# Layer 1's norms of seven token groups moved from a stage of their own into the slots of the first products

## What is computed

```python
def _layernorm(x, axis=-1, eps=1e-05):
    m = jnp.mean(x, axis=axis, keepdims=True)
    v = jnp.var(x, axis=axis, keepdims=True)
    return (x - m) / jnp.sqrt(v + eps)
...
xn = _layernorm(x)
s = _L1_attn_ref(xn, ...)      # rms norm of xn, gate, linear recurrence over the sequence
g = _silu(_L1_ffn_ref(xn, ...))
x = x + s * g
...
# _L1_attn_ref
xn = x * jax.lax.rsqrt(jnp.mean(x * x, axis=-1, keepdims=True) + EPS) * norm_w
u = (xn @ in_w.T + in_b) * sigmoid(xn @ gate_w.T + gate_b)
# b, c, d are linear in u; h[t] = a * h[t-1] + b[t]; s = x + (c * h + d) @ out_w.T + out_b
...
# _L1_ffn_ref: switch-head attention, 8 heads of 64, 5 experts each, the 3 best kept
ss_g, sd_g = sigmoid(x @ Ws) * top3_mask, sigmoid(x @ Wd) * top3_mask
q, k, v = (sum over 5 experts of (x @ W_expert) * gate)  # per head
attn = softmax(q * scale @ k.T); out = attn @ v
```

## Time and profile before

| | |
|---|---|
| three runs | 2652.54, 2656.14, 2662.70 us; median 2656.14 |
| profiled execution | 2662.89 us, its span 2661.1 us |
| PE busy | 2414.3 us (91% of the span), 13848 matmuls |
| DVE busy | 1819.5 us (68%) |
| ACT busy | 1290.4 us (48%) |
| POOL busy | 1252.5 us (47%) |
| chain that ended last | PE 34%, DVE 8%, ACT 4%, POOL 3% |

### The profile page before, as it was taken

How to read it: one execution, slowest core, us unless ns; L and a number is a source line. 1 busy time by engine, 2 the same in 40 slices (tenths; PEclk the granted TensorE clock), 3 DMA queues, 4 the chain that set the end, 5 groups by cost and what they waited for, 6 DMA issues and landing times.

```text
span 2661.1 us, 39371 instructions
## 1 busy us (share of the span) xinstructions
PE 2414.3 (91%) x13848; PEld 1556.9 (59%) x13848; DVE 1819.5 (68%) x3844; ACT 1290.4 (48%) x3379; POOL 1252.5 (47%) x1120
## 2 busy tenths in 40 slices
PE   6688699999999999996899999999989889898888
PEld 3476345555555555555455666666544567677776
DVE  5767676777877778764688787887665666555723
ACT  4577523343343433433456777766556335454442
POOL 1654077777777777773267334341000642333430
PEclk7799799999999999997899999999998998889998
DMA  4464300000000000002822223232101360212113
GB/s 175 138 202 149 106 1 1 1 1 1 1 1 1 1 1 1 1 1 82 218 64 72 73 73 84 74 83 59 33 1 41 104 179 22 68 31 63 42 44 101
DMA packets 189332, 158.81 MB, mean 60 GB/s; under 512 B 101408, under 2 KB 168480, under 8 KB 188320
## 3 DMA queue, kind: packets, MB, share of 16 engines
q1 hardware_dynamic: 166352, 90.25, 12.7%
q0 software_dynamic: 22784, 66.05, 8.0%
HBM read 126.49 MB, written 59.51 MB: 70 GB/s over the span
## 4 chain that ended last, share of the span: by engine, by line
PE 34%; DVE 8%; ACT 4%; POOL 3%; issue 2%; DMA 1%; SPq 0%; POOLq 0%; ACTq 0%; DVEq 0%
PE bank L65 29%; PE bank L2165 4%; POOL noted_rows L609 2%; DVE work L2100 1%; ACT work L2126 1%; ACT L3365 1%; DVE work L3481 1%; DVE work L3428 0%; DVE work L2144 0%; DVE work L3483 0%; DVE weights_odd L3481 0%; DVE work L3632 0%; DVE weights_even L3428 0%; PE bank L692 0%; DVE work L3597 0%
## 5 line engine op out<-in xcount | busy, mean ns | idle before, releaser
L1539 POOL TENSOR_TENSOR work<-work 128x512 f32<-128x512 f32 x384 | 501.4, 1306 | 256.3 <-DVE work L1531 235.7
L65 PE MATMUL bank<-work 64*128 64x256 f32 (+5 forms) x4384 | 592.6, 352 | 29.4 <-DVE work L3601 7.5
L65 PEld LDWEIGHTS bank<-work 64*128 64x128 f32 (+4 forms) x4384 | 413.6, 170 | 234.4 <-issue 141.0
L65 PE MATMUL bank<-weights_odd,normed_channels 128*128 128x512 f32 (+2 forms) x1088 | 512.2, 572 | 26.4 <-DVE work L1531 24.4
L1531 DVE TENSOR_TENSOR work<-bank,work 128x512 f32<-128x512 f32 x360 | 246.2, 685 | 154.7 <-PE bank L65 153.9
L2126 ACT ACTIVATE work<-bank,work 128x256 f32<-128x256 f32 x512 | 236.0, 473 | 224.1 <-DVE work L2113 224.1
L65 PEld LDWEIGHTS bank<-weights_odd,normed_channels 128*128 128x128 f32 x1088 | 172.1, 192 | 163.7 <-DVE work L1531 93.4
L1606 ACT ACTIVATE work<-bank,work 128x256 f32<-128x256 f32 x256 | 119.2, 470 | 290.5 <-DVE work L1593 290.4
L619 POOL DMA_INDIRECT weights_even<-in_L_Wx,expert_slots x112 | 113.8, 1016 | 254.6 <-PE bank L692 190.0
L2100 DVE TENSOR_REDUCE work<-bank 128x2 f32<-128x512 f32 x256 | 164.6, 684 | 72.9 <-PE bank L65 72.9
L3072 POOL TENSOR_TENSOR weights_odd<-weights_odd 128x512 f32<-128x512 f32 x40 | 52.9, 1323 | 281.6 <-ACT weights_odd L3067 281.6
(11 more groups left out here) (357 smaller groups left out, 4266.8 us busy)
## 6 DMA issues: line engine op xcount, KB each, us to landing
filter_matrices<-in_L_filters SPq DMA_DIRECT2D x24, 512.0 KB, 8.3
work<-filter_matrices SPq DMA_DIRECT2D x16, 768.0 KB, 6.2
weights_even<-noted_rows SPq DMA_DIRECT2D x56, 132.0 KB, 2.5
noted_rows<-in_empty SPq DMA_DIRECT2D x11, 660.0 KB, 9.2
noted_rows_in<-in_empty SPq DMA_DIRECT2D x8, 660.0 KB, 10.5
weights_odd<-noted_rows_in SPq DMA_DIRECT2D x40, 132.0 KB, 2.2
work<-token_rows SPq DMA_DIRECT2D x16, 256.0 KB, 3.3
token_rows_out<-in_zeros SPq DMA_DIRECT2D x6, 640.0 KB, 19.8
```

The source lines that it names most:

```text
L65: return pe.matmul(out, lhsT, rhs, start=first, stop=last, skip_group_check=True)
L1539: gp.tensor_tensor(self.sum_of(p), self.sum_of(p), self.product_of(p), ALU.add).then_inc(s["l1_add"], 1)
```

## The change

Group 0 alone is normed ahead of the slots. For groups 1 to 7 the centre product and the square stand at slots 1, 5, 9, ..., 25 (`CENTRED`), the variance product and the roots two slots later, DVE's two multiplications four slots later. The pieces that stood between the groups now follow group 0 directly. The squares go to the buffers `p` and `pt` of the attention instead of `prod`, since `prod` is in use now; the first scores and the first Exp of the softmax wait until all groups are done (`rms_done` at 8). `Norm`'s methods are split into one method for a group and step, with the same waits; Layers 0, 2 and 3 call them in the same order as before.

```diff
-        self.norm = Norm(k, n, self.prod, k.bank[3:7], (self.xr, self.norm_w))
+        self.norm = Norm(k, n, (*self.p, self.pt[0]), k.bank[3:7], (self.xr, self.norm_w))
...
+    def tensor_centre(self, pe, on, g):
...
+        on.wait_ge(s["ln_done"], base + g - 2)
+        if self.rms is not None:
+            on.wait_ge(s["rms_done"], g - 2)
+        mm(pe, self.cent[g % 3][:, :], k.center_w, cols(k.xT, g)).then_inc(s["ln_cent"], 1)
...
+    def tensor_variance(self, pe, on, g):
...
+        on.wait_ge(s["ln_sq"], base + g + 1)
+        on.wait_ge(s["ln_rstd"], 2 * (base + g) - 1)
...
+        mm(pe, self.var[:, :], k.mean_w, self.sq[g % 3]).then_inc(s["ln_var"], 1)
...
+    CENTRED = (1, 5, 9, 13, 17, 21, 25)
...
     def tensor_ahead(self, pe, on):
-
+        on.wait_ge(self.k.sem["residual"], GROUPS * self.n)
+        self.norm.tensor_centre(pe, on, 0)
         self.tensor_merge(pe, on)
-        for _ in range(3):
-            yield
+        self.norm.tensor_variance(pe, on, 0)
         self.tensor_route(pe, on, 0)
...
     def scalar_ahead(self, a, on):
...
+        a.preload_act_table_set(EXP_AND_LN)
+        on.wait_ge(s["residual"], GROUPS * self.n)
+        self.norm.scalar_square(a, on, 0)
+        self.norm.scalar_root(a, on, 0)
+        on.wait_ge(s["l1_small"], self.SMALL)
+        a.activation(self.a_log, self.a_log, ACT.Sigmoid, scale=-1.0).then_inc(s["l1_decay"], 1)
         self.scalar_route(a, on, 0)
         a.preload_act_table_set(EXP_AND_LN)
...
             if slot < L1_UNITS * BATCH:
                 self.tensor_product(pe, on, slot)
+            if (c := self.centred(slot)) is not None:
+                self.norm.tensor_centre(pe, on, c)
+            if (c := self.centred(slot, 2)) is not None:
+                self.norm.tensor_variance(pe, on, c)
...
+            if (c := self.centred(slot)) is not None:
+                self.norm.scalar_square(a, on, c)
+            if (c := self.centred(slot, 2)) is not None:
+                self.norm.scalar_root(a, on, c)
             if (p := self.turn_due(slot, 1)) is not None:
                 self.scalar_turn(a, on, p)
...
                 self.vector_product(v, on, slot)
+            if (c := self.centred(slot, 4)) is not None:
+                self.norm.vector_normed(v, on, c)
```

More of the change, by code:

```diff
@@ L192, in __init__ @@
         self.cent, self.var = banks[0:3], banks[3]
+    def tensor_centre(self, pe, on, g):
+        k, s, base = self.k, self.k.sem, GROUPS * self.n
+        if self.n == 0:
+            on.wait_ge(s[f"landed{g}"], 16)
+        on.wait_ge(s["residual"], base - GROUPS + g + 1)
+        on.wait_ge(s["ln_done"], base + g - 2)
[3 more added lines that the diff above has]
+    def tensor_variance(self, pe, on, g):
+        k, s, base = self.k, self.k.sem, GROUPS * self.n
+        on.wait_ge(s["ln_sq"], base + g + 1)
+        on.wait_ge(s["ln_rstd"], 2 * (base + g) - 1)
+        if self.rms is not None:
+            on.wait_ge(s["rms_root"], 2 * g - 1)
+        mm(pe, self.var[:, :], k.mean_w, self.sq[g % 3]).then_inc(s["ln_var"], 1)
     def tensor(self, pe, on, beside=iter(()), logits=None):
@@ L199, in tensor, with scalar_square, scalar_root @@
             if step < GROUPS:
[L200 to L206, removed]
+                self.tensor_centre(pe, on, step)
             next(beside, None)
             if 0 <= step - 1 < GROUPS:
[L209 to L214, removed]
+                self.tensor_variance(pe, on, step - 1)
             if logits is not None and step >= 3:
                 logits(pe, on, step - 3)
+    def scalar_square(self, a, on, g):
+        s, base = self.k.sem, GROUPS * self.n
+        on.wait_ge(s["ln_cent"], base + g + 1)
+        on.wait_ge(s["ln_done"], base + g - 2)
+        a.activation(self.sq[g % 3], self.cent[g % 3][:, :], ACT.Square).then_inc(s["ln_sq"], 1)
+    def scalar_root(self, a, on, g):
+        k, s, base = self.k, self.k.sem, GROUPS * self.n
+        on.wait_ge(s["ln_var"], base + g + 1)
+        a.activation(self.sq[g % 3], self.var[:, :], ACT.Ln, bias=k.eps_ln).then_inc(s["ln_rstd"], 1)
+        on.wait_ge(s["ln_rstd"], 2 * (base + g) + 1)
+        a.activation(self.sq[g % 3], self.sq[g % 3], ACT.Exp, scale=-0.5).then_inc(s["ln_rstd"], 1)
+        if self.rms is not None:
+            x = cols(self.rms[0], g)
+            a.activation(x, self.var[:, :], ACT.Ln, bias=k.eps_both, scale=1.0 + 1e-6).then_inc(s["rms_root"], 1)
+            on.wait_ge(s["rms_root"], 2 * g + 1)
+            a.activation(x, x, ACT.Exp, scale=-0.5).then_inc(s["rms_root"], 1)
     def scalar(self, a, on, beside=iter(())):
@@ L224, in scalar @@
             if step < GROUPS:
[L225 to L228, removed]
+                self.scalar_square(a, on, step)
             if step >= 1:
-                g = step - 1
-                on.wait_ge(s["ln_var"], base + g + 1)
-                a.activation(self.sq[g % 3], self.var[:, :], ACT.Ln, bias=k.eps_ln).then_inc(s["ln_rstd"], 1)
@@ L233, in scalar @@
[L233 to L239, removed]
@@ L240, in scalar, with vector_normed @@
-            next(beside, None)
+                self.scalar_root(a, on, step - 1)
+            next(beside, None)
+    def vector_normed(self, v, on, g):
+        k, s, base = self.k, self.k.sem, GROUPS * self.n
+        on.wait_ge(s["ln_rstd"], 2 * (base + g) + 2)
+        v.tensor_tensor(cols(k.xn, g), self.cent[g % 3][:, :], self.sq[g % 3], ALU.mult).then_inc(s["ln_done"], 1)
+        if self.rms is not None:
+            x, weight = self.rms
+            on.wait_ge(s["rms_root"], 2 * g + 2)
+            v.scalar_tensor_tensor(out=cols(x, g), in0=self.cent[g % 3][:, :], scalar=weight, in1=cols(x, g),
+                                   op0=ALU.mult, op1=ALU.mult).then_inc(s["rms_done"], 1)
@@ L242, in vector @@
     def vector(self, v, on, beside=iter(())):
-        k, s, base = self.k, self.k.sem, GROUPS * self.n
-        on.wait_ge(s["residual"], base)
+        on.wait_ge(self.k.sem["residual"], GROUPS * self.n)
         for g in range(GROUPS):
             next(beside, None)
[L247 to L253, removed]
+            self.vector_normed(v, on, g)
@@ L1578, in tensor_score @@
         m = h // 2
+        on.wait_ge(s["rms_done"], GROUPS)
         on.wait_ge(s["l1_turned"], 8 * bt + 8)
@@ L1755, in combined, with centred @@
         return None
+    CENTRED = (1, 5, 9, 13, 17, 21, 25)
+    def centred(self, slot, lag=0):
+        return self.CENTRED.index(slot - lag) + 1 if slot - lag in self.CENTRED else None
     def tensor_ahead(self, pe, on):
+        on.wait_ge(self.k.sem["residual"], GROUPS * self.n)
+        self.norm.tensor_centre(pe, on, 0)
         self.tensor_merge(pe, on)
-        for _ in range(3):
-            yield
+        self.norm.tensor_variance(pe, on, 0)
         self.tensor_route(pe, on, 0)
     def scalar_ahead(self, a, on):
[L1765 to L1768, removed]
+        s = self.k.sem
+        a.preload_act_table_set(EXP_AND_LN)
[4 more added lines that the diff above has]
+        a.activation(self.a_log, self.a_log, ACT.Sigmoid, scale=-1.0).then_inc(s["l1_decay"], 1)
         self.scalar_route(a, on, 0)
@@ L1773, in vector_ahead @@
         s = self.k.sem
+        on.wait_ge(s["residual"], GROUPS * self.n)
+        self.norm.vector_normed(v, on, 0)
         self.vector_merge(v, on)
-        for _ in range(5):
-            yield
         on.wait_ge(s["l1_decay"], L1_CLEARED - 2)
@@ L1780, in vector_ahead @@
         on.wait_ge(s["l1_decay"], L1_CLEARED)
-        for n, _ in enumerate(self.vector_route(v, on, 0)):
-            if n % 4 == 3:
-                yield
+        for _ in self.vector_route(v, on, 0):
+            pass
     def tensor(self, pe, on):
-        self.norm.tensor(pe, on, self.tensor_ahead(pe, on))
+        self.tensor_ahead(pe, on)
         beside = None
@@ L1812, in scalar @@
         s = self.k.sem
-        self.norm.scalar(a, on, self.scalar_ahead(a, on))
+        self.scalar_ahead(a, on)
         beside = None
@@ L1837, in vector @@
         s = self.k.sem
-        self.norm.vector(v, on, self.vector_ahead(v, on))
+        self.vector_ahead(v, on)
         beside, route = None, iter(())
```

## The result

Seven runs of the changed kernel have a median of 2674.4 us against 2662.7 us of seven runs of the kernel before; the ratio is **1.0055**, 95% interval 1.0032 to 1.0077. Forecast were 2671.5 us and, against 2656.14, a ratio of 1.0058. The measured ratio isn't the quotient of the two medians, which is 1.0044 (11.7 us). The changed kernel is slower beyond the interval; whether by more than 0.5%, the interval leaves open.

The account below looks back on a forecast made before the run. PE bounds the slots before the change, ACT with its table loads slots 5 to 30 after it. +11.0 (18.8 gained ahead, 29.8 lost in slots) + 4.9 clock - 0.5 POOL = +15.4 on 2656.1: 2671.5 us, range 2660 to 2680.

Parts of the forecast that it names:

- The prologue: Ahead of the slots: with only group 0 normed there, the first scaled product begins 18.8 us sooner.
- A group with four loads: ACT in the slots, groups 2 to 7: 3.20 us plus four table loads of 1.31 each, 8.46 us a group.
- the walk: Group-by-group times after the first scaled product, clock always high: slot 34 at 73.4 us, 11.0 us later than before.
- The ring of slot 25: C waits for the Identity's bank, the Identity for root 6: group 7's Ln comes 5.4 us after root 6.
- The clock: PE's lower clock after idling, ahead of variances of groups 5 to 7 and slot 32: 4.9 us, bounds 0 and 7.
- the 0.5 for POOL: At slot 34: a smaller backlog on POOL gives 0.5 us back.
- The two large items: Lower-clock charges: 1.5 us from C to group 7's variance, 1.6 us for slots 32 to 34.
- rival (c): After slot 34: the delay is regained; if half came back, 2663 us; chance 0.07.
- PE's busy share: Sign in the slots, 320 to 380 us: PE busy 60 to 75%.
- Rival (b): In the slots: loads don't bind, PE does with 12.0 us more; slot 34 6.7 us sooner, 2649.4 us; chance 0.08.

Follow-up runs that it names:

- e1: Changed kernel, ACT loading the joint Exp and Ln set again after both gate sigmoids of group 0's recurrence; ratio to the kernel before 0.9973.
- e2: Changed kernel, ACT loading the joint Exp and Ln set again after the first gate sigmoid (slot 4) alone; ratio to the kernel before 1.0046.
- e3: Kernel before the change without the joint set's preload behind the route's sigmoid, 15 more loads in all; ratio to the kernel before 1.0066.
- e6: Changed kernel with seven unread products in PE's idle time at slots 25 and 31; ratio to the kernel before 1.0062.
- e4: Changed kernel with group 0's first recurrence product C at the end of slot 28 instead of 25; ratio to the kernel before 1.0058.
- e7: e1 with DVE's merge ahead of group 0's multiplications and norms of groups 1 and 2 up to roots behind the route; ratio to before 0.9965.
- e8: Changed kernel with every centre product of groups 1 to 7 done twice; one run, slot 34 93.9 us after Layer 1's first centre product.
- e9: e1 with every centre product of groups 1 to 7 done twice; one run, slot 34 78.4 us after Layer 1's first centre product.

## Why the prediction was right, step by step

**The prologue** was to gain 18.8 us and gained 19.0. Its parts held too: the route's sigmoid ended 12.4 us after the first centre product, forecast 12.5, and the 14 operations took 7.1 against 7.3.

**A group with four loads** was to take 8.46 us. From the end of root 4 (355.66) to that of root 5 (364.03) it was 8.37 in the changed kernel, 10.9 with the turn and sigmoid of group 4 (11.1 in the walk), 8.9 with the turn of group 6 (9.1). That the loads are the cause, and not the further products or the clock, is shown by e1, e2 and e3 together.

**The ring of slot 25** was right in its size (5.4 us from root 6 to the Ln at the upper clock, 5.3 in e6), and only half right in its make-up: in e4, without C, the Ln still came 5.6 us behind root 6, since the scan of slot 24 holds product 27 back for 1.9 of them and the clock was low behind it.

**The clock** was right in the sum by luck, and partly wrong in place. With its 4.9 us, less the 0.5 for POOL, slot 34 was due 77.8 us after the first scaled product and came after 78.0. Nothing was lost ahead of the variances of groups 5 and 6, for which I charged 0.9 each: their Ln's start 0.02 us after their loads. The windows of the changed kernel show why. The first two are PE's idle time ahead of group 5's variance (PE starts it at 356.20) and that variance with the products behind it, the last is the variance of group 6 from 365.12 on:

```profile
354.00:356.00 2.00, 0.00 (x0) 0.00 (x0) 0.31 (x1) 1.99 (x3) 0.00 (x0) 1.00 0.00 0
356.40:359.50 3.10, 3.10 (x5) 1.20 (x5) 2.22 (x5) 3.06 (x4) 2.23 (x2) 0.62 0.00 0
364.50:367.00 2.50, 1.88 (x5) 0.93 (x6) 1.51 (x3) 2.47 (x4) 1.36 (x2) 1.00 0.00 0
```

The variance of group 5 took 1.16 us, at a clock of 0.92, and the lower level (0.50 from 357.2 to 360.6) met the products behind it, on which ACT doesn't wait. Ahead of group 6's variance PE idled for 1.8 us, and the clock stayed at 1.00. The two large items came about as charged, 1.5 for group 7 and 1.6 for slot 32: against the 5.3 and 6.6 us of e6 they are 1.6 each. The rest arose where I had charged nothing. Group 1's Ln was due at 4.8 us after the first scaled product and came at 6.3, because the clock was still low there (0.50 from 317 to 322); group 3's variance, at 0.59, made ACT wait 0.57. So 1.8 us that didn't come were made up by 2.1 that had not been charged. That a group's variance loses when PE has been idle ahead of it was a rule too simple: e2 and e4 have their lower clock in other places.

**Nothing was regained** (rival (c)) in the rest of Layer 1's products: +15.3 at slot 34 and +15.3 at slot 479. Of the signs that the prediction named, PE's busy share was off: from 8 to 68 us after the first scaled product, the prediction's 320 to 380, it was 80%, where 60 to 75 were written.

**Rival (b)**, PE as the bound, is what happens once the loads are gone. It gave 6.7 us sooner at slot 34 and e1 has 5.7. The Trainium skill's rule (ScalarE: Activation LUTs, Table sets: the hidden batching unit) that Ln and Exp share a set holds for e1, where the program names the joint set; left to itself the build loaded a set for each.

The step that mattered was one that isn't in the diff: the build's table loads, in the order of ACT's instructions. From the diff alone ACT had 3.2 us per group of four slots, and the change would have been forecast as a gain.

## What to carry to other kernels

A chain of Exp and Ln that is moved next to a sigmoid changes its own price. A preload of a set that holds both lasts until the next function from another set, and after that the build here placed one load for every Ln and every Exp. Look at the order of the changed program for table loads before costing anything on ACT, and set the joint table again behind each foreign function. Work moved "beside" other work is free only on engines that have idle time there: here PE's 14 products cost about what they are (e1 takes 13.2 us more than before from the first scaled product to slot 34, 12.0 were reckoned), so the best place for some of them was PE's idle time ahead of the slots (e7).

## What had not been expected of the hardware

More work made the stage shorter. With seven further products of 0.86 us, e8 reached slot 34 3.8 us sooner than the changed kernel: one of them fell between 309 and 312 us, ahead of slot 2, where PE otherwise idles, and the granted clock was 1.00 in slots 0 to 5, where the changed kernel has 0.64; this gave 2.8 us. Another 1.7 came between root 6 and the Ln of group 7 (5.2 us against 6.9, at 1.00 against 0.75). e9 shows the first of the two again. The second stands on one execution, and e2 has the same 5.2 without added products. In the changed kernel the lower level cost ACT nothing where it met group 5, since it came behind the variance. Where exactly the clock falls after an idle PE, these runs don't settle.
